# The second attention's output projections: element 2's moved into groups 13 and 14, three quarters of element 3's into group 15

## The reference, cut to what matters

```python
def _L2_xattn_ref(x, latents, attention_mask, q_w, q_b, kv_w, kv_b, out_w, out_b, postnorm_w, mlp_w1, mlp_b1, mlp_w2, mlp_b2):
    B, P, K, H, NH = (4, 512, 64, 512, 16)
    DH = H // NH
    residual = latents
    h = jnp.concatenate([x, latents], axis=1)
    q = (latents @ q_w + q_b).reshape(b, k_len, NH, DH)
    kv = (h @ kv_w + kv_b).reshape(b, p + k_len, NH, DH, 2)
    attn = jnp.einsum('bkhd,bnhd->bhkn', q, kmat) / DH
    attn = jnp.where(full_mask[:, None, None, :], attn, -jnp.inf)
    attn = jax.nn.softmax(attn.astype(jnp.float32), axis=-1).astype(q.dtype)
    attn_out = jnp.einsum('bhkn,bnhd->bkhd', attn, v).reshape(b, k_len, H)
    attn_out = attn_out @ out_w + out_b + residual
    out = rmsnorm(attn_out, postnorm_w)
    out = jax.nn.gelu(out @ mlp_w1 + mlp_b1) @ mlp_w2 + mlp_b2
    return out + residual
```

## Time and profile before

| what | value |
|---|---|
| median of 3 runs | 2831.62 us (2829.5 to 2832.07) |
| profiled execution, its own time | 2831.26 us |
| its span | 2829.2 us |
| mean granted clock of PE | 0.972 |
| PE, DVE, ACT, POOL busy | 94%, 52%, 28%, 13% |

### The profile page before, as it was taken

How to read it: one execution, slowest core, us unless ns; L and a number is a source line. 1 busy time by engine, 2 the same in 40 slices (tenths; PEclk the granted TensorE clock), 3 DMA queues, 4 the chain that set the end, 5 groups by cost and what they waited for, 6 DMA issues and landing times. The chain is left out here.

```text
span 2829.2 us, 30362 instructions
## 1 busy us (share of the span) xinstructions
PE 2663.9 (94%) x12328; PEld 1942.8 (69%) x12328; DVE 1462.0 (52%) x2282; ACT 782.2 (28%) x1363; POOL 381.7 (13%) x246
## 2 busy tenths in 40 slices
PE   9999999999799999889999999879999889799999
PEld 7778777877678887645444444358888656578887
DVE  6465566555753443335445454375344586763442
ACT  4322243223221111115344343431111243321110
POOL 0000000000120000015243343331000310120000
PEclk9999999999999999899999999889999999999999
DMA  4101110110100001211112121020000100100001
GB/s 188 60 30 42 49 60 30 45 45 1 63 16 16 30 1 55 87 48 48 48 48 63 39 62 49 24 108 30 16 15 1 68 1 0 64 1 30 30 1 60
DMA packets 35556, 118.28 MB, mean 42 GB/s; under 512 B 8021, under 2 KB 8150, under 8 KB 25946
## 3 DMA queue, kind: packets, MB, share of 16 engines
q1 hardware_dynamic: 35418, 116.35, 12.4%
HBM read 81.18 MB, written 7.34 MB: 31 GB/s over the span
## 5 line engine op out<-in xcount | busy, mean ns | idle before, releaser
L1541 DVE TENSOR_REDUCE l_top<-l_slot 128x1 f32<-128x512 f32 x256 | 170.4, 679 | 192.2 <-PE l_slot L1352 191.5
L1491 ACT ACTIVATE l_weighed<-l_across 128x512 f32<-128x512 f32 (+1 forms) x320 | 183.0, 594 | 300.2 <-PE l_across L1374 296.6
L389 PE MATMUL l_wide<-l_key_map,l_norm 128*128 128x260 f32 x1024 | 235.3, 383 | 2.7 <-ACT l_norm L544 2.3
L389 PEld LDWEIGHTS l_wide<-l_key_map,l_norm 128*128 128x128 f32 x1024 | 191.8, 190 | 32.1 <-ACT l_norm L544 2.7
L1222 POOL TENSOR_TENSOR l_paired<-l_weighed 128x2048 f32<-128x2048 f32 x32 | 145.5, 4546 | 396.7 <-ACT l_weighed L1491 336.4
L1374 PE MATMUL l_across<-l_q_stack,l_k_stack 99*128 99x512 f32 (+1 forms) x320 | 186.8, 588 | 12.1 <-ACT l_weighed L1491 9.1
L725 DVE TENSOR_TENSOR x<-l_added,x 128x512 f32<-128x512 f32 x128 | 87.1, 687 | 82.0 <-PE l_added L131 60.5
L1374 PEld LDWEIGHTS l_across<-l_q_stack,l_k_stack 99*128 99x128 f32 (+1 forms) x320 | 59.2, 186 | 97.6 <-issue 61.6
L1352 PE MATMUL l_slot<-l_k_stack,l_q_stack 97*128 97x512 f32 x256 | 112.2, 439 | 14.3 <-DMA l_k_stack<-l_k_parts 6.4
L2319 ACT ACTIVATE l3m_hidden<-l3m_up,columns 128x512 f32<-128x512 f32 x64 | 44.1, 690 | 272.8 <-PE l3m_up L131 262.0
L2319 ACT ACTIVATE l0m_hidden<-l0m_up,columns 128x512 f32<-128x512 f32 x64 | 44.2, 692 | 271.0 <-PE l0m_up L131 258.5
(11 more groups left out here) (379 smaller groups left out, 5971.4 us busy)
## 6 DMA issues: line engine op xcount, KB each, us to landing
l_k_stack<-l_k_parts SPq DMA_DIRECT2D x192, 72.0 KB, 2.0
l_q_stack<-l_q_parts SPq DMA_DIRECT2D x192, 64.0 KB, 2.0
l_wk<-in_weights SPq DMA_DIRECT2D x9, 1024.0 KB, 4.7
l_wv<-in_weights SPq DMA_DIRECT2D x9, 1024.0 KB, 4.8
l_wo<-in_weights SPq DMA_DIRECT2D x9, 1024.0 KB, 4.8
l_wqT<-in_weights SPq DMA_DIRECT2D x8, 1024.0 KB, 6.9
l0m_raw<-in_weights SPq DMA_DIRECT2D x8, 1024.0 KB, 4.7
l2m_raw<-in_weights SPq DMA_DIRECT2D x8, 1024.0 KB, 4.8
```

Source lines behind the costliest of these rows:

```text
L389: last = pe.matmul(wide[:, j, 0:W], norm[:, k, at:at + P], key_map[:, k, b, :, :].rearrange("p h c -> p (h c)"), start=k == 0, stop=k == K ...
L1491: act.activation(weighed[0:height(c), (CHUNKS * g + c) % RING, j, :], across[0:height(c), use % 2, :], ACT.Exp)\
L1541: dve.tensor_reduce(top[:, t, j:j + 1], slot[:, i % 2, :], AX.X, ALU.max, negate=True).then_inc(s["top_ready"], 1)
```

## The change

The output projection of element 2 no longer runs as a block after group 11. Its 16 products run in groups 13 and 14, one a step, in steps 0 to 3 and 8 to 11, a token tile for each four, all in the bank `l_work`, which the projections no longer need there. DVE adds a tile to `rows` after the maxima of steps 5 and 13. Element 3's projection is cut by head groups: the products of head groups 0 to 2 for all four tiles run in steps 0 to 11 of group 15, in four banks; after the last normalisation the four products of head group 3 follow. `mixed` has a second buffer, so that element 3's groups can be written while element 2's are still read. POOL's additions of input and bias for element 3 move from group 12 to group 15, between its two pairs, behind the store of element 2, which SP now issues at group 14, after the last stack.

```diff
-        mixed = n.sbuf(f"{tag}_mixed", [P, GROUPS, S], F32, mem)
+        mixed = n.sbuf(f"{tag}_mixed", [P, 2, GROUPS, S], F32, mem)
...
+        LAST_BANK = (slot_bank[0], slot_bank[1], slot_bank[2], work[:, :])
+        TAIL = ALL - GROUPS + 1
...
-                if g % GROUPS == GROUPS - 1 and b + 1 < B:
+                if g == ALL - 2:
+                    sp.wait_ge(s["out_added"], TPB * (B - 1))
+                    sp.dma_start(n.dram["l2_rows"][:, (B - 2) * TPB:(B - 1) * TPB, :], rows[:, :, :]).then_inc(s["rows_stored"], 16)
+                elif g % GROUPS == GROUPS - 1 and b + 2 < B:
...
+                if g == ALL - 1:
+                    add_bias(b)
                 add_pair(g, 1)
...
+                if g % GROUPS == 0 and b + 1 < B:
+                    add_bias(b)
...
-                    if b + 1 < B and t < 3:
+                    if t < 3:
                         pe.wait_ge(s["values_out"], CHUNKS * (b + 1) + t + 3)
...
+            def out_product(b, t, m, bank):
+                return pe.matmul(bank, mixed[:, b % 2, m, t * P:(t + 1) * P], wo[:, m, :], start=m == 0, stop=m == GROUPS - 1)
+
+            def late_out(g, step):
+                if step % 8 >= GROUPS or step >= TILES_OF:
+                    return
+                t, m = 2 * (g - TAIL) + step // 8, step % 8
+                if m == 0:
+                    if t:
+                        pe.wait_ge(s["out_added"], TPB * (B - 2) + t)
+                    else:
+                        pe.wait_ge(s["mixed_ready"], GROUPS * (B - 1))
+                        pe.wait_ge(s["k1_out"], ALL)
+                last = out_product(B - 2, t, m, work[:, :])
+                if m == GROUPS - 1:
+                    last.then_inc(s["out_done"], 1)
+
+            def last_out(step):
+                if step >= TPB * (GROUPS - 1):
+                    return
+                m, t = step // TPB, step % TPB
+                if step == 0:
+                    pe.wait_ge(s["top_ready"], TILES_OF * ALL)
+                    pe.wait_ge(s["ctx_top_ready"], 4 * ALL)
+                    pe.wait_ge(s["out_added"], TPB * (B - 1))
+                if t == 0:
+                    pe.wait_ge(s["mixed_ready"], GROUPS * (B - 1) + m + 1)
+                out_product(B - 1, t, m, LAST_BANK[t])
+
+            def finish_out():
+                pe.wait_ge(s["mixed_ready"], ALL)
+                for t in range(TPB):
+                    out_product(B - 1, t, GROUPS - 1, LAST_BANK[t]).then_inc(s["out_done"], 1)
...
-                        pe.wait_ge(s["out_added"], TPB * (g // GROUPS))
+                        pe.wait_ge(s["out_added"], TPB * min(g // GROUPS, B - 2))
...
+                        elif g + 1 < ALL:
+                            late_out(g, TPB * c + j)
+                        else:
+                            last_out(TPB * c + j)
...
-                    if g + 1 < ALL:
-                        project_values(g // GROUPS + 1)
-                    project_out(g // GROUPS)
+                    b = g // GROUPS
+                    if b + 1 < B:
+                        project_values(b + 1)
+                    if b + 2 < B:
+                        project_out(b)
+            finish_out()
...
-                if b and m == 0:
-                    dve.wait_ge(s["out_done"], TPB * b)
-                dve.tensor_tensor(mixed[:, m, :], gathered[:, :], inverse[:, :], ALU.mult).then_inc(s["mixed_ready"], 1)
+                if b >= 2 and m == 0:
+                    dve.wait_ge(s["out_done"], TPB * (b - 1))
+                dve.tensor_tensor(mixed[:, b % 2, m, :], gathered[:, :], inverse[:, :], ALU.mult).then_inc(s["mixed_ready"], 1)
...
+                    if TAIL <= g < ALL - 1 and i in (5, 13):
+                        add_out(B - 2, 2 * (g - TAIL) + i // 8, work[:, :])
...
-                    add_out(b)
+                    for t in range(TPB):
+                        if b + 2 < B:
+                            add_out(b, t, slot_bank[OUT_BANK[t]])
+                        elif b + 1 == B:
+                            add_out(b, t, LAST_BANK[t])
```

23 lines of the change are left out of this document (11 added, 12 removed).

## The result

| | before | changed |
|---|---|---|
| median of the runs | 2831.62 us (2829.5 to 2834.5, n = 5) | 2814.24 us (2812.64 to 2820.59, n = 5) |
| ratio | | 0.9946, 95% interval 0.9933 to 0.9958 |
| profiled execution: time, span | 2831.26, 2829.2 us | 2814.24, 2812.1 us |
| mean granted clock of PE | 0.972 | 0.977 |

The change makes the kernel 17.4 us faster by the medians, and 0.54% by the ratio. The forecast was 18.7 us and 2813 us, with a range of 2808.5 to 2823. The total came out close, but two of its four terms did not, and a part of the difference between the two profiles lies in code that the change doesn't touch.

The account below looks back on a forecast made before the run. PE, busy 94% of the span, was taken as the bound, with idle places and a low clock in the stage's tail. Terms -14.0 + 1.8 + 3.8 - 10.3 = -18.7 us gave 2812.6, against the median 2813; range 2808.5 to 2823.

Parts of the forecast that it names:

- A: Block after group 11: its sixteen products leave, 13.44 us, and group 12's first logits come sooner, 0.55; -14.0 us.
- B: Groups 13 and 14 take eight products and two row additions each: 29.7 us a group, +1.8 us for both.
- in groups 10 to 12 it held at 1.00 with two thin steps: Argument against rival 1: groups 10 to 12 kept a granted clock of 1.00 despite two thin steps.
- rival 1: Clock falls in thin steps 4 to 7 of groups 13 or 14: some 5 us a group, 2818 or 2823; chance 0.24.
- group by group comparison: Groups 13 and 14 priced from group 10's 28.68 us, which carries nearly the same load: 29.7 us each.
- C: Group 15 takes twelve products of element 3 in steps 0 to 11, at 1.10 us a step and full clock: +3.8 us.
- POOL's margin: Group 15: one microsecond of cover hides POOL's moved additions before PE's second pair sum.
- D: Stage's end: twelve of sixteen output products no longer run after the last normalisation, -10.3 us.
- only those first four remain: Step of D: at the stage's end the first four products stay, which took 5.13 us before; twelve go, -10.3 us.
- Rivals 2 to 4: 2: late products' cover missing, 2824.5 us, 0.08; 3: POOL late in group 15, 2818, 0.05; 4: half clock, 2881, 0.03.
- The rule on the clock: Groups 13 to 15: if only long idle gaps lose the clock, they keep it full and the forecast sum stands.

Follow-up runs that it names:

- element 2's part alone: The change with only element 2's projection moved into groups 13 and 14, element 3's whole at the end, against the kernel before: 2819.19 us, ratio 0.9968.
- element 3's part alone: The change with only element 3's projection moved into group 15, element 2's the block after group 11, against the kernel before: 2823.88 us, ratio 0.9981.

## Why the prediction was right, and where not

**A, -14.0.** As forecast: the block of 13.44 us is gone, and the time from the first "across" to the first logits fell from 1.55 to 1.01 us.

**B, forecast +1.8, measured +6.7** (31.41 + 32.82 against 57.55). The step "in groups 10 to 12 it held at 1.00 with two thin steps", which I took as evidence that the new groups keep the clock, failed. Four thin steps are what rival 1 described, and it came true in both groups, at 1.7 and 3.1 us instead of the 5 it was priced at, since the clock came back after 3.5 and some 6 us. My forecast had 0.58 for a full clock and gave rival 1 only 0.24. The rest of B was right: the kernel with element 2's part alone, where the clock held, has 29.76 and 29.78 us where the group by group comparison gave 29.7.

**C, forecast +3.8, measured +3.7.** Twelve steps at a pitch of 1.09 us, the full clock, and POOL's margin of 1.10 us all came out as worked out. The kernel without POOL's moved additions has the same group.

**D, forecast -10.3, measured -8.9.** The step "only those first four remain" was short by their clock: PE is busy with the four for 6.72 us, where element 3's part alone has 5.14 and the prediction had taken 5.13. In that kernel the stretch is 10.05 us and the term is -10.5, so this too is clock. It isn't a matter of too few products: behind the same idle time of 4.24 us the clock was back for the third product in one kernel and in the course of the last in the other, and the prediction took the value of one profile as fixed.

**The sum.** -14.0 + 6.7 + 3.7 - 8.9 = -12.5 us for the stage, not -18.7. In the first pair of profiles the total came near the forecast because 3.4 us were gained in front of that stretch and 1.2 behind it, 2.3 of them in group 3, which the change doesn't touch. So the mechanism held, two terms were mis-sized by 4.9 and 1.4 us through the clock, and that the total landed within 1.3 us of the forecast is luck. In its second set of runs the change was 16.3 us below the kernel before (2812.22 against 2828.56), and the ratios of both sets, 0.9946 and 0.9944, stand for 15 to 16 us. The second pair of profiles has -12.0 for the same stretch. How much of the difference between 12 and 16 belongs to the change can't be told from these profiles, in which the unchanged code before the stretch and behind it moves by 6 and 8 us.

**The signs that the prediction named.** Its own conditions for being wrong were a group above 33 us or a clock below 0.9, a wait for POOL, or less than 14 us at the stage's end. None of them came, but the first was missed by little (32.82 us, 0.90): the mark had been set too far out to catch a loss of 5 us. The last was met by luck too: the stage's end moved by 15.9 us, 3.4 of them gained in front; the stretch itself became only 12.5 us shorter.

**The rule on the clock.** TensorE: Matmul & The Clock Gate (HAM oscillation) in the Trainium skill puts the loss of the clock down to long idle gaps, such as a DMA wait. Group 3 agrees in kind, if with shorter gaps: the clock fell behind DMA waits of 1.51 to 2.00 us. Groups 13 and 14 disagree: the clock fell behind gaps of 1.06 and 1.05 us, and in group 13 of the kernel before behind 0.91 us. The same page of the Trainium skill, in its section on psum-queue depth-cycling, says that many small idles make the clock swing. The rows of these two groups agree with that better: the kernels with thin runs of four and seven steps lost the clock, those with no two thin steps in a row kept it in groups 13 and 14. The same thin run of four steps kept it in one kernel (29.76 us), and why it did is open.

**Rivals 2 to 4** are excluded: 2 by the 29.76 us at full clock, 3 by POOL's 1.10 us of idle time, 4 by clocks of 0.95, 0.90 and 1.00. Rival 1 came true in part.

## What to carry to other kernels

Try to spread work that fills idle places, and compare it with putting it into neighbouring steps. In this kernel neighbouring steps made PE and DVE wait in turn, and the run of thin steps cost PE its clock in four of five profiles; spread, the clock held in all four. Price a moved product at the pitch of a group that already carries such products, and then ask of every run of steps without one what the clock does there. Before a gain is put down to an edit, look at how much the stretches that it doesn't touch have moved between the two profiles.

## What the runs showed of the hardware that was not expected

- **The clock depends on more than the group.** The same instructions in groups 13 and 14 took 31.41 and 32.82, 31.42 and 32.75, and 31.44 and 31.24 us in three profiles, and 29.76 and 29.78 in a kernel whose code differs only after them.
- **A gap is not enough.** A PE wait of 1.02 us with no two thin steps in a row before it left the clock at full speed. One of 1.06 us behind four thin steps was followed by a product of 1.87 instead of 1.02 us, and one of 1.02 us behind the same four thin steps, with element 2's part alone, by a product of 1.02.
- **A POOL instruction can hold DVE up for most of its length.** Four scalings of 128x512 took 1.68 us alone and 7.60 us beside POOL's split of a weight tile. A scaling of 128x4, normally 0.17 us, took 3.82 us in the kernel before and 4.20 in the changed one when it met the same kind of split in the last MLP. SBUF — State Buffer (Who interferes with whom) in the Trainium skill says that the two share a pair of ports that one instruction holds to its end while the other fully blocks; the rows agree, as the 7.60 us are the scalings' own 1.68 and most of POOL's 1.89 and 4.55.
